# Mixture-of-experts tail of a two-layer gated block: expert tiles of 256 rows in two blocks, and two accumulating scatters in a row without a wait between them

## The reference

```python
scores = sigmoid(xf @ gate_w.T)                # xf: 8192 tokens x 256, 8 experts
_, sel = top_k(scores + expert_bias, 2)        # 2 experts for each token
def body(acc, (e, wu, wd)):
    w_t = sum(where(sel == e, top_scores, 0))  # weight of this expert for each token
    h = square(relu((xf * w_t) @ wu.T))        # 256 -> 512
    return acc + h @ wd.T                      # 512 -> 256
x = x + tanh(g_ffn[1]) * _moe(layernorm(x))
```

## Time and profile before

| | us |
|---|---|
| median of 3 runs | 2578.39 |
| lowest and highest run | 2574.0, 2589.82 |
| span of the profiled execution | 2582.9 |
| part 2 in it, first scatter issued to last landed | about 1955 to 2581 |
| PE, DVE, ACT, POOL busy over the span | 2207.2, 1309.8, 751.3, 954.7 |

### The profile page before, as it was taken

The page is one execution under the profiler, slowest core; times in us unless marked ns, Lnnn a source line. Parts: engine busy times, 40 slices in busy tenths (PEclk is TensorE's granted clock), DMA queues, the critical chain, the costliest instruction groups (busy, mean ns, idle before and its releaser), DMA issues.

```text
span 2582.9 us, 44103 instructions
## 1 busy us (share of the span) xinstructions
PE 2207.2 (85%) x13970; PEld 1819.5 (70%) x14003; DVE 1309.8 (51%) x3668; ACT 751.3 (29%) x1509; POOL 954.7 (37%) x1330
## 2 busy tenths in 40 slices
PE   2899999999999999999999899999809888888884
PEld 1677777777777777777777777777607766677763
DVE  1456555565555556556554655656454433343331
ACT  2122222222222222222222222222234444444432
POOL 1234343343434335343442434434222333333333
PEclk7799998999898999999999999999958999999997
DMA  4000000000000000000010000000053333333332
GB/s 111 2 9 28 27 8 27 16 27 8 27 27 8 27 16 27 8 27 27 9 34 8 27 12 23 27 16 24 15 167 61 60 57 57 57 57 57 59 53 29
DMA packets 93781, 88.28 MB, mean 34 GB/s; under 512 B 26896, under 2 KB 87312, under 8 KB 93752
## 3 DMA queue, kind: packets, MB, share of 16 engines
q0 software_dynamic: 26160, 35.87, 8.1%
q1 hardware_dynamic: 67592, 52.04, 7.4%
HBM read 43.48 MB, written 44.39 MB: 34 GB/s over the span
## 4 chain that ended last, share of the span: by engine, by line
PE 51%; DMA 18%; issue 12%; DVE 7%; POOL 5%; ACT 5%; SPq 1%; POOLq 0%; DVEq 0%; ACTq 0%
PE scores L1086 30%; DMA out<-y,ids 17%; PE bank L1086 16%; POOL sorted_rows L665 3%; PE bank L1154 2%; DVE t_lo L891 1%; DVE biased L968 1%; ACT t_hi L744 1%; ACT routed L779 1%; POOL rstd L612 1%; PE scores L1211 1%; DVE e L965 1%; POOL kb_hi L630 1%; DMA raw<-w_down_t 1%; ACT neg_mx L754 1%
## 5 line engine op out<-in xcount | busy, mean ns | idle before, releaser
L693 POOL DMA_INDIRECT out<-y,ids x136 | 211.6, 1556 | 464.8 <-ACT y L803 281.6
L612 POOL TENSOR_TENSOR rstd<-var,half_power 128x2 f32<-128x2 f32 x128 | 90.0, 703 | 681.0 <-DVE var L878 680.3
L1086 PE MATMUL scores<-vb,pr 128*128 128x136 f32 x2048 | 280.8, 280 | 0.7 <-ACT pr_rest L765 0.7
L891 DVE TENSOR_TENSOR t_lo<-bank,t_hi 128x512 fp32r<-128x512 f32 x192 | 132.1, 688 | 257.6 <-ACT t_hi L744 255.1
L1086 PEld LDWEIGHTS scores<-vb,pr 128*128 128x128 f32 x2048 | 259.2, 191 | 4.5 <-ACT pr_rest L765 0.9
L1086 PE MATMUL scores<-q_hi,kb_hi 128*128 128x256 f32 (+1 forms) x640 | 223.2, 349 | 34.4 <-ACT neg_mx L754 34.4
L1086 PE MATMUL scores<-neg_mx,expand 8*128 8x256 f32 (+1 forms) x640 | 246.5, 385 | 0.0
L744 ACT ACTIVATE t_hi<-bank 128x512 fp32r<-128x512 f32 x192 | 114.6, 597 | 441.7 <-PE bank L1154 441.6
L1070 DVE SCALAR_TENSOR_TENSOR h<-scores,relu 128x512 f32<-128x512 f32 x136 | 94.1, 692 | 274.6 <-ACT relu L797 268.6
L941 DVE TENSOR_REDUCE mx<-scores 128x8 f32<-128x512 f32 x256 | 169.6, 683 | 122.3 <-remote 81.5
L1086 PE MATMUL scores<-up_hi,xt_hi 128*128 x272 | 121.1, 445 | 82.8 <-DVE xt_lo L1064 82.6
(11 more groups left out here) (221 smaller groups left out, 5744.4 us busy)
## 6 DMA issues: line engine op xcount, KB each, us to landing
xe<-sorted_rows SPq DMA_DIRECT2D x136, 128.5 KB, 2.1
x<-x_rows SPq DMA_DIRECT2D x32, 256.0 KB, 2.9
out<-x_end SPq DMA_DIRECT2D x32, 256.0 KB, 3.0
raw<-w_up_t SPq DMA_DIRECT2D x8, 512.0 KB, 4.6
raw<-w_down_t SPq DMA_DIRECT2D x8, 512.0 KB, 4.5
ctx<-ctx_t SPq DMA_DIRECT2D x32, 77.0 KB, 2.7
out<-y,ids POOLq DMA_INDIRECT x136, 3.8
sorted_rows<-routed,place POOLq DMA_INDIRECT x128
```

Source lines behind the costliest of these rows:

```text
L612: pool.tensor_tensor(rstd[u][:], var[u][:], half_power[:], ALU.pow).then_inc(sem(f"rstd_ready{u}"), 1)
L693: pool.indirect_dma_start(out=acc, out_offset=bass.IndirectOffsetOnAxis(ap=ids[j][:], axis=0), in_=y[j][:], in_offset=None, compute_op=ALU ...
L891: dve.tensor_tensor(t_lo[u][:].rearrange("p k t -> p (k t)"), bankC[:], t_hi[u][:].rearrange("p k t -> p (k t)"), ALU.subtract).then_inc(s ...
L1086: last = pe.matmul(dst, w, m, start=n == 0, stop=n == len(pairs) - 1)
```

## The change

A tile is now 256 rows (ROWS) in NB = 2 blocks of 128, and block is what a tile was before. There are NT = 2 * 8192 / 256 + 8 = 72 tiles and so BLOCKS = 144 blocks. SP loads both blocks of a tile with one transfer; the ring has 4 tiles instead of 8 (RING). POOL waits for the earlier scatters at even blocks only. A tile's rows belong to one expert, so its two blocks add to different rows of `acc`. The zero rows behind each expert are 256, sent with 18 indirect transfers; the spare rows of `acc` are 256. The waits of `ids` and `y` for a scatter are rounded up to a whole tile.

```diff
+NB = 2
+ROWS = NB * P
-CAP = TOK + P
+CAP = TOK + ROWS
-NT = 2 * TOK // P + E
+NT = 2 * TOK // ROWS + E
+BLOCKS = NB * NT
+RING = DEEP // NB
...
-        xe = [sb2(f"xe{i}", [P, ROW]) for i in range(DEEP)]
+        xe = [sb2(f"xe{i}", [P, NB, ROW]) for i in range(RING)]
...
-            sp.dma_start(acc[TOK:TOK + P, :], zero_rows[:, 0:D]).then_inc(sem("acc_zero"), 16)
+            sp.dma_start(acc[TOK:TOK + ROWS, :].rearrange("(b p) d -> p b d", p=P), zero_rows[:, :, 0:D]).then_inc(sem("acc_zero"), 16)
...
-            sp.wait_ge(sem("ended"), 16 * (E + 1))
+            sp.wait_ge(sem("ended"), 16 * NB * (E + 1))
...
-            def load(k, j):
-                if j >= DEEP:
-                    sp.wait_ge(sem("xe_used"), k * DEEP + (j - DEEP + 1))
-                    sp.wait_ge(sem("ids_ready"), k * DEEP + (j - DEEP + 1))
+            def load(k, i):
+                if i >= RING:
+                    sp.wait_ge(sem("xe_used"), k * DEEP + NB * (i - RING + 1))
+                    sp.wait_ge(sem("ids_ready"), k * DEEP + NB * (i - RING + 1))
                 carrier(sp)
-                sp.dma_start(xe[j % DEEP][:], sorted_rows[bass.ds(row, P), :]).then_inc(sem(f"xe_in{j % DEEP}"), 16)
+                sp.dma_start(xe[i % RING][:], sorted_rows[bass.ds(row, ROWS), :].rearrange("(b p) d -> p b d", p=P))\
+                  .then_inc(sem(f"xe_in{i % RING}"), 16)
...
-            for e in range(E + 1):
+            for e in range(NB * (E + 1)):
                 pool.indirect_dma_start(out=sorted_rows, out_offset=bass.IndirectOffsetOnAxis(ap=ends[:, e:e + 1], axis=0),
-                                        in_=zero_rows[:], in_offset=None).then_inc(sem("ended"), 16)
+                                        in_=zero_rows[:, e // (E + 1), :], in_offset=None).then_inc(sem("ended"), 16)
...
-            with pool.Fori(0, NT // DEEP) as k:
+            with pool.Fori(0, BLOCKS // DEEP) as k:
                 for j in range(DEEP):
                     pool.wait_ge(sem("y_ready"), k * DEEP + (j + 1))
                     pool.wait_ge(sem("ids_ready"), k * DEEP + (j + 1))
-                    pool.wait_ge(sem("added"), k * (DEEP * 16) + j * 16)
+                    if j % NB == 0:
+                        pool.wait_ge(sem("added"), k * (DEEP * 16) + j * 16)
...
-                    act.wait_ge(sem("added"), k * (DEEP * 16) + (j + 1 - DEEP) * 16)
+                    act.wait_ge(sem("added"), k * (DEEP * 16) + ((j - DEEP) // NB + 1) * NB * 16)
...
-            after(dve.tensor_scalar(ends_f[:, 0:E], run[:], own_row[:, 0:1], None, ALU.add))
-            after(dve.tensor_scalar(ends_f[:, E:E + 1], own_row[:], float(IDLE), None, ALU.add))
+            for b in range(NB):
+                after(dve.tensor_scalar(ends_f[:, b, 0:E], run[:], own_row[:, 0:1], float(b * P), ALU.add, ALU.add))
+                after(dve.tensor_scalar(ends_f[:, b, E:E + 1], own_row[:], float(IDLE + b * P), None, ALU.add))
...
-                    dve.wait_ge(sem("added"), k * (DEEP * 16) + (j + 1 - DEEP) * 16)
-                dve.tensor_copy(ids[j % DEEP][:], xe[j % DEEP][:, D:ROW]).then_inc(sem("ids_ready"), 1)
+                    dve.wait_ge(sem("added"), k * (DEEP * 16) + ((j - DEEP) // NB + 1) * NB * 16)
+                dve.tensor_copy(ids[j % DEEP][:], xe[j // NB % RING][:, j % NB, D:ROW]).then_inc(sem("ids_ready"), 1)
...
-                pe.wait_ge(sem(f"xe_in{j % DEEP}"), k * 16 + (j // DEEP + 1) * 16)
+                pe.wait_ge(sem(f"xe_in{j // NB % RING}"), k * 16 + (j // DEEP + 1) * 16)
```

More of the change, by code:

```diff
@@ L86, in build @@
     acc = out
-    sorted_rows = nc.dram_tensor("sorted_rows", [IDLE + P, ROW], F32, kind="Internal").ap()
+    sorted_rows = nc.dram_tensor("sorted_rows", [IDLE + ROWS, ROW], F32, kind="Internal").ap()
     bias_line = nc.dram_tensor("bias_line", [H, LINE], F32, kind="Internal").ap()
@@ L199, in build @@
         own_row = sb1("own_row", [P, 1])
-        ends_f = sb1("ends_f", [P, E + 1])
-        ends = sb1("ends", [P, E + 1], U32)
+        ends_f = sb1("ends_f", [P, NB, E + 1])
+        ends = sb1("ends", [P, NB * (E + 1)], U32)
         count = sb1("count", [P, E])
@@ L210, in build @@
                                   xn[1][:].rearrange("p c d -> p (c d)")[0:1, NT:2 * NT])
-        zero_rows = sb1("zero_rows", [P, ROW])
+        zero_rows = sb1("zero_rows", [P, NB, ROW])
         wf_gate = sb1("wf_gate", [P, 1])
@@ L444, in in_order @@
                 step(0, j)
-            with fori(0, NT // DEEP - 2) as k:
+            with fori(0, BLOCKS // DEEP - 2) as k:
                 for j in range(DEEP, 2 * DEEP):
                     step(k, j)
-            k = NT // DEEP - 2
+            k = BLOCKS // DEEP - 2
             for j in range(DEEP, 2 * DEEP):
@@ L542, in _ @@
                              a[name][n // 2].rearrange("(k p) n -> p k n", p=P)).then_inc(sem(f"raw_in{n % 4}"), 16)
-            def load(k, j):
-                if j >= DEEP:
-                    sp.wait_ge(sem("xe_used"), k * DEEP + (j - DEEP + 1))
-                    sp.wait_ge(sem("ids_ready"), k * DEEP + (j - DEEP + 1))
+            def load(k, i):
+                if i >= RING:
+                    sp.wait_ge(sem("xe_used"), k * DEEP + NB * (i - RING + 1))
+                    sp.wait_ge(sem("ids_ready"), k * DEEP + NB * (i - RING + 1))
                 carrier(sp)
-                row = sp.value_load(tile_table[0:1, bass.ds(k * DEEP + j, 1)], min_val=0, max_val=IDLE)
-                sp.dma_start(xe[j % DEEP][:], sorted_rows[bass.ds(row, P), :]).then_inc(sem(f"xe_in{j % DEEP}"), 16)
[L553 to L557, removed]
+                row = sp.value_load(tile_table[0:1, bass.ds(k * RING + i, 1)], min_val=0, max_val=IDLE)
+                sp.dma_start(xe[i % RING][:], sorted_rows[bass.ds(row, ROWS), :].rearrange("(b p) d -> p b d", p=P))\
+                  .then_inc(sem(f"xe_in{i % RING}"), 16)
+            for i in range(RING):
+                load(0, i)
+            with sp.Fori(0, NT // RING - 1) as k:
+                for i in range(RING):
+                    load(k, RING + i)
         @block.gpsimd
@@ L576, in _ @@
                       allow_small_or_imprecise_dtypes=True).then_inc(sem("consts"), 1)
-            pool.memset(zero_rows[:, 0:D], 0.0).then_inc(sem("zero_ready"), 1)
-            pool.iota(zero_rows[:, D:ROW], pattern=[[0, 1]], base=TOK, channel_multiplier=1,
+            pool.memset(zero_rows[:, :, 0:D], 0.0).then_inc(sem("zero_ready"), 1)
+            pool.iota(zero_rows[:, :, D], pattern=[[P, NB]], base=TOK, channel_multiplier=1,
                       allow_small_or_imprecise_dtypes=True).then_inc(sem("zero_ready"), 1)
@@ L694, in _ @@
                                             in_=y[j][:], in_offset=None, compute_op=ALU.add).then_inc(sem("added"), 16)
-            pool.wait_ge(sem("added"), NT * 16)
+            pool.wait_ge(sem("added"), BLOCKS * 16)
         @block.scalar
@@ L1022, in _ @@
             after(dve.tensor_copy(tile_no[:], tile_table[:, 0:NT]))
-            after(dve.tensor_scalar(ends_f[:, 0:E], run[:], own_row[:, 0:1], None, ALU.add))
-            after(dve.tensor_scalar(ends_f[:, E:E + 1], own_row[:], float(IDLE), None, ALU.add))
-            dve.tensor_copy(ends[:], ends_f[:]).then_inc(sem("ends_ready"), 1)
+            for b in range(NB):
+                after(dve.tensor_scalar(ends_f[:, b, 0:E], run[:], own_row[:, 0:1], float(b * P), ALU.add, ALU.add))
+                after(dve.tensor_scalar(ends_f[:, b, E:E + 1], own_row[:], float(IDLE + b * P), None, ALU.add))
+            dve.tensor_copy(ends[:], ends_f[:].rearrange("p b e -> p (b e)")).then_inc(sem("ends_ready"), 1)
             after(dve.tensor_tensor(count[:], run[:], first_row[:], ALU.subtract))
-            after(dve.tensor_scalar(count_i[:], count[:], float(P - 1), None, ALU.add))
-            after(dve.tensor_scalar(tiles_i[:], count_i[:], P.bit_length() - 1, None, ALU.arith_shift_right))
+            after(dve.tensor_scalar(count_i[:], count[:], float(ROWS - 1), None, ALU.add))
+            after(dve.tensor_scalar(tiles_i[:], count_i[:], ROWS.bit_length() - 1, None, ALU.arith_shift_right))
             after(dve.tensor_copy(tiles_f[:], tiles_i[:]))
@@ L1032, in _ @@
                 after(dve.tensor_tensor(until[:, e:e + 1], until[:, e - 1:e], tiles_f[:, e:e + 1], ALU.add))
-            after(dve.scalar_tensor_tensor(out=shift[:, 1:E], in0=until[:, 0:E - 1], scalar=float(-P), in1=first_row[:, 1:E],
+            after(dve.scalar_tensor_tensor(out=shift[:, 1:E], in0=until[:, 0:E - 1], scalar=float(-ROWS), in1=first_row[:, 1:E],
                                            op0=ALU.mult, op1=ALU.add))
@@ L1037, in _ @@
             after(dve.tensor_tensor(step_of[:, 1:E - 1], shift[:, 2:E], shift[:, 1:E - 1], ALU.subtract))
-            after(dve.tensor_scalar(rows_f[:], tile_no[:], float(P), None, ALU.mult))
+            after(dve.tensor_scalar(rows_f[:], tile_no[:], float(ROWS), None, ALU.mult))
```

(8 more changed lines are left out.)

## The result

The changed kernel takes 2503.25 us (median of 4 runs, 2497.49 to 2519.88); the kernel before, run beside it, 2584.11 (4 runs, 2574.0 to 2595.98). The ratio is 0.9693, with a 95% interval of 0.9632 to 0.9754: 3.1% faster. 2505.8 was forecast.

A forecast was written before the change was run, and what follows sets the result against it. Part 2 was taken as bound by scatter landings, 4.606 us a tile, then by PE at 3.74: 118 us saved, 30, 11 and 3 paid, 73 left, giving 2505.8 us on the runs' scale, range 2488 to 2550.

The forecast's parts named there:

- What bound before: Part 2 before the change: each accumulating scatter waits for the previous landing, 4.606 us a tile; PE waits too.
- The pair of scatters: POOL in part 2: the odd scatter no longer waits for a landing, so a pair takes 6.97 us, 3.49 a block.
- PE is late next, at 3.74: Part 2 after the change: PE binds at 3.74 us a block, 7.48 for two, more than the scatters' 6.97.
- the run ahead of the first tiles: Head of part 2 before: eight free buffers let PE run ahead of the scatters, showing its own pace, 3.74 us.
- Rival C: Part 2: PE's pace is not kept, handovers from ACT and DVE cost 0.25 us more a block; 2541 us, chance 0.07.
- More blocks: Part 2: 144 blocks instead of 136 cost 8 x 3.74 = 29.9 us on PE's path.
- More zero rows: Before part 2's weights load: 9 further indirect transfers at 1.27 us, 11.4 us on the path.
- PE's clock: Part 2: 3 us added for lost clock, as part 1 was granted 0.97 on average against 1.00.
- The sum: Whole kernel: 118 us saved, 30, 11 and 3 paid, 73 left; span 2510, 2505.8 on the runs' scale.
- Loads and rounded waits: Part 2: 257 KB loads, taken as 2.9 us, are hidden; rounded ids and y waits have 10 us spare, nothing added.
- Rival A: Part 2: scatters slow each other, odd landings 4.95 us, pair 8.12, scatters bind again; around 2548 us, chance 0.12.
- Rival B: Part 2: POOL cannot ready a second scatter while one is in flight, pair 9.21 us; 2626.5 us, chance 0.06.

The follow-up runs named there:

- the other order: Kernel before with the turn of block j+2 placed ahead of up(j+1) on all engines: 2581.65 us, ratio 1.0027.
- the kernel in which scatters bind: Changed kernel with the turn of block j+2 ahead of up(j+1) and the down product in one of three passes: 2462.17 us in one run.
- the early weights: Changed kernel with zero rows, their places and table scratch outside part 1, so SP loads weights before waiting for table and zero scatters: 2479.52 us, ratio 0.9632.
- the two kernels with one down pass: Down product in one of its three passes, in the kernel before and in the changed kernel: 2571.15 us and 2491.72 us, one run each.

## Why the prediction was right, point by point

- **What bound before.** Shown: with a third of the down product the kernel before keeps 4.6 us a tile, with the other order too.
- **The pair of scatters.** The forecast's 6.97 us is 6.86 in the kernel in which scatters bind. Two of its terms were off in opposite directions: the gap ahead of the odd scatter is 0.30 us, the lower bound, where I took 0.8; and the landing of an odd scatter that begins 1.86 us behind an even one is 4.1 to 4.2 us, where I took 3.8. In the changed kernel itself the odd one begins 2.7 us behind and 4.58 us pass to the next even one, 3.8 of landing and the gap of 0.79, so the term holds there.
- **PE is late next, at 3.74.** Measured 3.72 in a pass of the loop, 3.68 over all. The size was right and so was its source, the run ahead of the first tiles. The step's reading of it, "so there PE is the bound", was only half of the truth: PE's own work is 3.49 us; the ring through ACT and DVE holds it at 3.65, and the reads of the expert add the last 0.07. Busy 36.41 of 36.89 us had hidden this, since stretched matmuls count as busy: six up matmuls take 1.57 us where they had to wait for the low half and 1.40 elsewhere, and four turns of h 0.65 behind a read and 0.44 without. Rival C named the handovers, but as a loss in addition to 3.74; they were inside it.
- **More blocks.** 29.9 us, forecast and measured.
- **More zero rows.** 21.52 - 10.11 = 11.41 us more between first and last begin, 11.4 forecast, and on the path, as the early weights show. From the routed rows to the first y it became only 7.8 us later (63.96 before, 71.76 after). The other 3.6 came back because PE's clock rose sooner: before, three up products ran at 2.94 us ahead of the first y; after, one at 2.94 and then 1.66. That is luck of the two executions and not the change: in the two kernels with one down pass, where two ran at 2.94 each, the first y comes 60.69 and 73.28 us behind the routed rows, 12.6 apart.
- **PE's clock.** The 3 us for it were not needed: 1.00 from 2000 to 2400. Part 1 had 0.96 in that execution, so the reason given for the term, that PE would be as busy as in part 1, does not carry over. Where the clock was lower in this stretch PE was less busy: 0.97 at 337.70 us of 400 with the wait put back, 0.94 at 274.31 in the kernel before with one down pass. What lowered it there stays open; others as idle had 1.00 (341.31 us in the kernel before).
- **The sum.** That 2505.8 lies so near 2503.25 is partly luck. The gain was forecast as 72.6 us and is 80.9 (83.6 by the stretches). From the routed rows the forecast comes to 619.9 us and 609.2 were measured. The differences: the first y 3.6 earlier and the 3 us for the clock, both told above; the 143 intervals 526.8 instead of 534.8, 8.0 less; and from the last y to the end 10.6 us instead of 7.0, 3.5 more, since the last two y come after 2.10 and 1.73 us and the scatters fall behind them (the rest is rounding). And the kernel before, at 2578.39 when the forecast was made, has 2584.11 in the comparison.
- **Loads and rounded waits.** No row of the changed kernel puts PE's idle time down to a load; the kernel with the wait put back has the same 4.6 us distance as before, with loads of 257 KB in it.
- **Rival A** has a grain of truth, 0.3 to 0.4 us on the landing of an odd scatter that begins 1.86 us behind an even one, and not the 4.95 of its price. The Trainium skill (DMA: Bandwidth & Descriptors, Latency and other measured facts), which lets the fixed cost rise with load, agrees in direction only: 77 GB/s in that kernel, 71 in the changed one, where the landing is still 3.8. But in that same kernel, at the same 77 GB/s, the even scatters land after 3.81 us and only the odd ones after 4.14 (medians of 59 and 58 between 2000 and 2400 us). So the mean load alone does not explain it. Whether the neighbour just ahead does, or what else moves beside the second of a pair, no run here tells. **Rival B** is excluded: 1.86 us from even to odd.

## What to carry to other kernels

When transfers must be ordered only because they may touch the same rows, group the work so that neighbours cannot, and wait once a group; count what the grouping adds (52 us here) against what the dropped waits give (135.7, both by the stretches). Behind the removed bound look for the next two, not one: take out a part of the next engine's work and see whether the pace follows; if it does not, the chain of that run names a ring over several engines, and here one swapped pair of lines in the written order opened it, worth 24 us by itself and 31.6 with the reads that it hid. The same swap was worth nothing before. To tell two such causes apart, look at which instruction begins late: a gap ahead of turning h was the read, a late up product the ring.

## What was not expected of the hardware

In the kernel with early weights, POOL makes the zero scatters ready while DVE splits the weights. Timeline of POOL, and of DVE in the same stretch:

```profile
1887.96 0.96 POOL L682 DMA_INDIRECT sorted_rows<-zero_rows,ends  x1 [0.31 <-issue]
1889.22 1.92 POOL L682 DMA_INDIRECT sorted_rows<-zero_rows,ends  x1 [0.30 <-issue]
1891.45 1.84 POOL L682 DMA_INDIRECT sorted_rows<-zero_rows,ends  x1 [0.30 <-issue]
...
1889.08 1.22 DVE L1060 TENSOR_TENSOR up_lo<-raw,up_hi 128x1024 fp32r<-128x1024 f32 x1 [2.42 <-issue]
1891.22 1.22 DVE L1060 TENSOR_TENSOR down_lo<-raw,down_hi 128x1024 fp32r<-128x1024 f32 x1 [0.92 <-issue]
```

A scatter that begins inside one of these DVE instructions takes 1.4 to 1.9 us instead of 0.96 and ends 0.82 to 0.85 us after it (1889.08 + 1.22 = 1890.30, and 1889.22 + 1.92 = 1891.14). Six of the 18 do, and no other is longer than 0.96. That is how a POOL held until DVE is done would look. The Trainium skill (SBUF — State Buffer, Who interferes with whom) says that a DVE instruction with two SBUF inputs contends with a GpSimd instruction that reads SBUF; the split reads two SBUF tiles, and the indirect transfer takes its rows' numbers from SBUF, so the rows agree. The accumulating scatters, beside DVE instructions with one input in PSUM, stay at 1.55 to 1.57 us.

This hold is not what made the early weights gain less than hoped: the last zero row is sent at 1907.56, long before the last weights are split at 1924.5. SP asks for the first weights 23 us earlier than in the changed kernel, counted from the last routed rows (2.7 against 25.7 us behind them). From there to the first turn it takes 41.5 us (1883.06 to 1924.6) against 31.9 (1934.60 to 1966.5): 9.6 are lost. The chain in this stretch goes through the transfers of the weights, and they are slower: a piece of down weights lands after 6.9 us (median) against 4.7. The 18 zero scatters move beside them here and not there; that they are the reason is likely, but was not tried by itself. Another 1.3 us went to PE's clock, two up products at 2.94 us ahead of the first y against one. So 12 of the 23 came back.
